# Pre-norm decoder layer with routed experts: the last stage takes x already turned and split, with other buffers, banks and orders

## The reference

```
x = x + self_attention(layernorm(x))                       # 16 heads, Wqkv 512x1536, Wo 512x512
x = x + layernorm(rs * cross_attention(layernorm(x), ctx)) # 16 heads, Wq, Wk, Wv, Wo 512x512
x = x + ffn(layernorm(x))

ffn(x):                       # 2048 tokens
  scores = softmax(x @ gate.T)                             # 64 experts, 8 groups
  keep the 3 best groups, of them the 6 best experts: topk_w, topk_i
  slot = expert * 192 + min(position in the expert, 191)
  buf[slot] = x[token]                                     # 64 x 192 rows
  out = (silu(buf @ Wg.T) * (buf @ Wu.T)) @ Wd.T           # 352 hidden an expert
  y = sum over the 6 choices of out[slot] * topk_w
  shared = (silu(x @ Sg.T) * (x @ Su.T)) @ Sd.T            # 704 hidden
  return y + shared
```

## Time and profile before

| | us |
|---|---|
| median of 3 runs | 1537.34 |
| the profiled execution | 1540.01 |
| its span, first to last instruction | 1538.3 |
| TensorE busy (share of the span) | 1464.2 (95%) |
| VectorE busy | 1115.0 (72%) |
| ScalarE busy | 941.6 (61%) |
| GpSimd busy | 688.1 (45%) |

### The profile page before, as it was taken

How to read it: one execution, slowest core, us unless ns; L and a number is a source line. 1 busy time by engine, 2 the same in 40 slices (tenths; PEclk the granted TensorE clock), 3 DMA queues, 4 the chain that set the end, 5 groups by cost and what they waited for, 6 DMA issues and landing times.

```text
span 1538.3 us, 30281 instructions
## 1 busy us (share of the span) xinstructions
PE 1464.2 (95%) x10344; PEld 1216.4 (79%) x10344; DVE 1115.0 (72%) x1959; ACT 941.6 (61%) x1769; POOL 688.1 (45%) x830
## 2 busy tenths in 40 slices
PE   6999999899999979689999999999999999999988
PEld 4788887678888867578888898888888888876766
DVE  5677676636788788777777777777777777757756
ACT  4556566644656556677777777778777777741110
POOL 2122124342232146355556555555555555347763
PEclk9999999999999999889999999999999999999999
DMA  6012122242121141299877788777887788567664
GB/s 212 1 63 83 37 75 70 73 124 70 56 90 43 43 125 49 88 330 342 283 269 268 264 295 275 271 265 268 298 271 269 268 272 299 193 216 246 191 185 151
DMA packets 116629, 280.25 MB, mean 182 GB/s; under 512 B 17984, under 2 KB 23104, under 8 KB 116544
## 3 DMA queue, kind: packets, MB, share of 16 engines
q1 hardware_dynamic: 98800, 228.25, 43.7%
q0 software_dynamic: 15360, 50.34, 10.7%
q10 hardware_dynamic: 2384, 0.53, 0.2%
HBM read 235.69 MB, written 43.38 MB: 181 GB/s over the span
## 4 chain that ended last, share of the span: by engine, by line
PE 50%; issue 3%; DVE 3%; DVEq 1%; ACT 0%; DMA 0%; SPq 0%
PE e_gu L2615 18%; PE e_gu L2618 9%; PE e_dn_rest L2644 6%; PE e_tr L49 3%; PE e_dn_main L41 3%; PE e_dn_main L43 3%; PE e_dn_main L42 3%; DVE h_acc L2909 1%; DVEq L2938 1%; PE h_dn L41 1%; PE h_dn L42 1%; PE h_dn L43 1%; PE h_gt L41 0%; PE h_gt L43 0%; PE h_gt L42 0%
## 5 line engine op out<-in xcount | busy, mean ns | idle before, releaser
L2377 POOL TENSOR_TENSOR e_hid<-e_h_raw,e_hid 128x256 fp32r<-128x256 f32 (+1 forms) x128 | 128.9, 1007 | 225.7 <-ACT e_hid L2443 225.7
L2615 PE MATMUL e_gu<-e_xT_hi_lo,e_wu 128*128 128x384 f32 (+1 forms) x768 | 223.9, 346 | 0.0
L2615 PE MATMUL e_gu<-e_xT_hi_lo,e_wg 128*128 128x384 f32 (+1 forms) x768 | 221.8, 343 | 0.4 <-issue 0.4
L2618 PE MATMUL e_gu<-e_xT_hi_lo,e_wu 128*128 128x192 f32 (+1 forms) x768 | 157.8, 260 | 0.0
L2385 POOL TENSOR_TENSOR e_wd<-e_raw_d,e_wd 96x512 fp32r<-96x512 f32 x64 | 132.6, 2071 | 55.5 <-ACT e_wd L2427 55.5
L2618 PE MATMUL e_gu<-e_xT_hi_lo,e_wg 128*128 128x192 f32 (+1 forms) x768 | 152.2, 253 | 0.0
L2519 DVE TENSOR_TENSOR e_total<-e_gu,e_low 128x384 f32<-128x384 f32 x192 | 106.1, 553 | 48.3 <-issue 38.9
L2508 DVE TENSOR_TENSOR e_wg<-e_raw_g,e_wg 128x1408 fp32r<-128x1408 f32 x64 | 104.1, 1627 | 45.8 <-ACT e_wg L2418 45.3
L2618 PEld LDWEIGHTS e_gu<-e_xT_hi_lo,e_wg 128*128 128x128 f32 (+1 forms) x768 | 135.2, 180 | 0.0
L2618 PEld LDWEIGHTS e_gu<-e_xT_hi_lo,e_wu 128*128 128x128 f32 (+1 forms) x768 | 134.8, 179 | 0.0
L2439 ACT ACTIVATE e_low<-e_gu 128x384 f32<-128x384 f32 x192 | 93.9, 489 | 59.9 <-issue 49.1
(11 more groups left out here) (427 smaller groups left out, 3941.2 us busy)
## 6 DMA issues: line engine op xcount, KB each, us to landing
e_raw_g<-in_L_ffn_Wg_dram SPq DMA_DIRECT2D x64, 704.0 KB
e_raw_u<-in_L_ffn_Wu_dram SPq DMA_DIRECT2D x64, 704.0 KB
e_raw_d<-in_L_ffn_Wd_dram SPq DMA_DIRECT2D x64, 512.0 KB
y_dram<-e_y_main SPq DMA_DIRECT2D x64, 256.0 KB
e_raw_d<-in_L_ffn_Wd_dram SPq DMA_DIRECT2D x64, 192.0 KB
y_dram<-e_y_rest SPq DMA_DIRECT2D x64, 128.0 KB
s_xr<-in_x_dram SPq DMA_DIRECT2D x16, 256.0 KB
x_dram<-s_x SPq DMA_DIRECT2D x16, 256.0 KB, 2.6
```

What stands on the lines that cost most here:

```text
L2377: pool.tensor_tensor(hid[b][1][:, part, :], h_raw[g.odd][b][:, part, 0:P], hid[b][0][:, part, :].bitcast(F32), ALU.subtract).then_inc(s_hl, 1)
L2615: pe.matmul(gu[(b + c) % 2][0:n, at, 0:2 * CAP], w[b][0][:, k, m:m + n], xT[:, :, k, toks], start=k == 0, stop=False)
L2618: ins = pe.matmul(gu[(b + c) % 2][0:n, at, 0:CAP], w[b][1][:, k, m:m + n], xT[:, 0, k, toks], start=False, stop=k == KC - 1)
```

## The change

- SP stores in cross-attention the two halves of the turned x of the 12 tiles outside AHEAD to `xfT_dram` (two DMAs of 256 KB a tile), and ScalarE's next copy into the single buffer waits for them.
- The last stage loads these halves (two DMAs of 1 MB a turn) into `h_xT` in place of loading xf, turning it and splitting it. The first turn's load is issued in the last expert turn.
- The last matmul of a down tile runs on all 128 rows, with `h_sd`'s first half zeroed in the 64 rows that had been left out.
- Three buffers for gathered rows in place of two, four down banks in place of two.
- VectorE's order of sums and finishes in the last stage is another.
- In every expert half ScalarE splits part 1 of the down weights behind the first SiLU in place of behind the second, and GpSimd's low half of it comes ahead of both low halves of the hidden. In the last expert turn TensorE makes the rest of the down products ahead of the last down product.

```diff
+        def turned_before(t):
+            return len([m for m in range(t) if m // QT != AHEAD])
...
+            def store_turned(t):
+                if t < LAST - 2:
+                    sp.wait_ge(s_er[0], exchanged(0, ("xf", t)))
+                else:
+                    sp.wait_ge(s_fl, t - LAST + 3)
+                at = t % QT * P
+                for half in range(2):
+                    sp.dma_start(route["xfT"][t // QT][half][:, :, at:at + P], fT[half][:].bitcast(F32)).then_inc(s_stT, 16)
...
             for t in range(BATCH + 2):
+                if t >= 3 and (t - 3) // QT != AHEAD:
+                    store_turned(t - 3)
                 if t >= 2:
                     store_x3(t - 2)
...
                 if t:
                     act.wait_ge(s_lg, t)
+                if t and t // QT != AHEAD:
+                    act.wait_ge(s_stT, 32 * turned_before(t))
...
                 if not first:
                     store_main(g.last(), 0)
+                if last:
+                    ahead.load_turned(sp, 0)
...
             def hidden_lo(g, b):
+                down_lo(g, b)
                 for i, part in enumerate(PARTS):
...
-                    if i == 0:
-                        down_lo(g, b)
 
             def down_lo(g, b):
-                pool.wait_ge(s_dh[b], 2 * g.n + 2)
+                pool.wait_ge(s_dh[b], 2 * g.n + 1)
...
                 silu(g, b, 0)
+                d_hi(g, b, 1)
                 low_part(g, b, 1)
...
                 d_hi(g, b, 0)
                 silu(g, b, 1)
-                d_hi(g, b, 1)
                 hidden_hi(g, b, 1)
...
-            ahead.turn_tokens(pe, 0, 2, QT)
+            down_rest(pair(turns - 1))
             down_main(pair(turns - 1), 1)
-            down_rest(pair(turns - 1))
...
+    def load_turned(sp, p):
+        if p == 0:
+            sp.wait_ge(*free["gate_up_before_last"])
+        elif p == 1:
+            sp.wait_ge(*free["raw_down_of_last"])
+        else:
+            sp.wait_ge(s_gu, SCN * (p - 1))
+        for half in range(2):
+            sp.dma_start(xT[p % 2][half][:].bitcast(F32), turned[order[p]][half]).then_inc(s_xt[p % 2], 16)
...
         def gather(n):
-            b = n % 2
-            if n >= 2:
-                pool.wait_ge(s_acc[b], TOPK * (n // 2))
+            b = n % ROWS
+            if n >= ROWS:
+                pool.wait_ge(s_acc[b], TOPK * (n // ROWS))
...
+        dve.memset(sd[0][low_rows, FULL, :].bitcast(F32), 0.0).then_inc(s_wz, 1)
+        early_half, late_half = range(TOPK // 2), range(TOPK // 2, TOPK)
         chunks(0, {2: (0, 0), 3: (0, 1), 4: (1, 0)})
         routed(1, late_half)
         finish(0)
...
-        routed(4)
-        chunks(1, {0: (5, 0), 1: (5, 1), 2: (6, 0), 3: (6, 1), 4: (7, 0)})
-        routed(7, late_half)
+        routed(4, early_half)
+        chunks(1, {0: (4, 1), 1: (5, 0), 2: (5, 1), 3: (6, 0), 4: (6, 1)})
+        routed(7)
         finish(4)
+        finish(5)
         routed(8)
-        finish(5)
-        routed(9)
         finish(6)
         finish(7)
-        routed(10)
-        chunks(2, {1: (11, 0), 2: (11, 1), 3: (12, 0), 4: (12, 1)})
+        routed(9)
+        chunks(2, {1: (10, 0), 2: (10, 1), 3: (11, 0), 4: (11, 1)})
         for c in range(SCN):
             hidden_lo(3, c)
         finish(8)
+        routed(12)
+        finish(9)
         routed(13)
-        finish(9)
-        routed(14)
         finish(10)
         finish(11)
+        routed(14)
         routed(15)
...
                 if n < 2:
                     pe.wait_ge(*free[("main_bank", "rest_bank")[n]])
-                else:
-                    pe.wait_ge(s_o[n % 2], n // 2)
-                toks, bank = slice(t * P, (t + 1) * P), dn[t % 2]
+                elif n >= QT:
+                    pe.wait_ge(s_o[n % 2], (n - QT) // 2 + 1)
+                toks, bank = slice(t * P, (t + 1) * P), dn[t]
...
-                pe.matmul(bank[:], hid_half[late][high_rows, toks], sd[0][high_rows, FULL, :], start=False, stop=True
-                          ).then_inc(s_dn, 1)
+                pe.matmul(bank[:], hid_half[late][:, toks], sd[0][:, FULL, :], start=False, stop=True).then_inc(s_dn, 1)
```

More of the change, by code:

```diff
@@ L920 @@
 AHEAD_SUMS = 6
+ROWS = 3
 COPIED = 4
@@ L2420, in d_hi @@
             def d_hi(g, b, part):
-                if part == 0:
+                if part == 1:
                     act.wait_ge(s_ld[g.odd][b], 32 * (g.uses + 1))
-                f = before(g, b, 2)
-                if f is not None:
-                    act.wait_ge(s_dm, 2 * f[0].n + b + 1)
+                    f = before(g, b, 2)
+                    if f is not None:
+                        act.wait_ge(s_dm, 2 * f[0].n + b + 1)
                 rows, cs = ((P, slice(0, 2)), (96, slice(2, 3)))[part]
@@ L2684, in sb, with shared_programs @@
         return ctx.enter_context(nc.sbuf_tensor("h_" + name, shape, dt))
-    return dict(xf=sb("xf", [P, QT, H]), ones=sb("ones", [P, 1]),
-                idx=[sb(f"idx{b}", [P, TOPK], U32) for b in range(2)], w_t=[sb(f"w_t{b}", [P, TOPK]) for b in range(2)],
-                carry=[sb(f"carry{b}", [P, 1]) for b in range(2)])
-def shared_programs(nc, sems, mine, own, raw, loaded, xf, x3, y_in, out, weight, slot, ident, experts, ahead_hidden):
+    return dict(ones=sb("ones", [P, 1]),
+                idx=[sb(f"idx{b}", [P, TOPK], U32) for b in range(ROWS)], w_t=[sb(f"w_t{b}", [P, TOPK]) for b in range(ROWS)])
+def shared_programs(nc, sems, mine, own, raw, loaded, turned, x3, y_in, out, weight, slot, experts, ahead_hidden):
     order = [q for q in range(BATCH // QT) if q != AHEAD] + [AHEAD]
@@ L2731, in shared_programs @@
         raw_hid = sb("raw_hidden", [P, SCN, QT * P])
-        xf_sb, idx, w_t, carry, ones = (own[k] for k in ("xf", "idx", "w_t", "carry", "ones"))
+        yk.append(sb("yk2", [P, TOPK * H]))
+        idx, w_t, ones = (own[k] for k in ("idx", "w_t", "ones"))
         gt, up = [None, None], [None, None]
@@ L2745, in shared_programs @@
         s_rh = sem("raw_hidden_loaded")
[L2746 to L2749 removed]
+        s_idx = [sem(f"idx_ready{b}") for b in range(ROWS)]
+        s_yk = [[sem(f"rows_gathered{b}_{k}") for k in range(TOPK)] for b in range(ROWS)]
+        s_wt = [sem(f"weights_ready{b}") for b in range(ROWS)]
+        s_acc = [sem(f"routed_sum_step{b}") for b in range(ROWS)]
         s_o = two(sem, "out_ready")
@@ L3050, in feed_forward @@
         experts = expert_programs(nc, sems, wg_in, wu_in, wd_in, xf, table, y, ident, shared_in, raw, loaded, shared)
-        shared_programs(nc, sems, shared, own, raw, loaded, xf, x3, y, out, weight, slot, ident, experts, ahead_hidden)
+        shared_programs(nc, sems, shared, own, raw, loaded, turned, x3, y, out, weight, slot, experts, ahead_hidden)
         ctx.callback(end_phase, nc, sems)
@@ L3117, in build @@
         table = ctx.enter_context(nc.sbuf_tensor("table", [E, CAP + P - REST], F32))
+        xfT = nc.dram_tensor("xfT_dram", [BATCH // QT, 2, P, KC * QT * P], F32, kind="Internal").ap()
+        turned = [[xfT[q, half].rearrange("p (k s) -> p k s", k=KC) for half in range(2)] for q in range(BATCH // QT)]
         ahead_hidden = nc.dram_tensor("hidden_dram", [SCN * P, QT * P], F32, kind="Internal").ap()
```

80 lines of the change are left out of this document (21 added, 59 removed).

## The result

The changed kernel took 1518.83 us (median of 4 runs, 1517.48 to 1519.98), the kernel before 1536.87 beside it (4 runs): a ratio of 0.989, interval 0.9874 to 0.9906. In a later comparison on another chip the same changed kernel took 1529.73 (6 runs, 1526.88 to 1533.2) against 1539.82: 0.9937, interval 0.9919 to 0.9955. It is faster in both; the size of the gain, 18 or 10 us, is what the experiments had to explain.

The account below looks back on a forecast made before the run. TensorE was taken as the bound, a leaky one in the last stage; 27.0 us less, 7.7 more in the loop and 0.5 for the first pair, net 18.8, gave 1521.2 profiled, 1518 median; range 1507 to 1531.

Parts of the forecast that it names:

- the loop: Expert loop: GpSimd's earlier subtraction holds VectorE, so TensorE stops about 0.25 us, 31 times: +7.7 us.
- the first pairs: First expert pair: the down weights are waited for earlier, 0.5 us more.
- Transposes: Last expert turn and last stage: six packets leave TensorE, 4.7 us less, and their own waits, 2.4 us.
- stops: Last stage: the other 10.1 us of TensorE stops nearly vanish, 0.9 us kept, gain 9.2 us.
- clock: Last stage: the slow clock behind two TensorE stops goes with them, gain 3.5 us.
- padding: Down tiles of the last stage: three gaps become 0.24 us, 0.37 us a tile, 16 tiles, gain 5.9 us.
- restarts: TensorE's second matmul behind each stop or transpose packet comes 0.1 us later; about 13 go, gain 1.3 us.
- two buffers, a late gather, a late sum, a late product, a TensorE stop: Last stage: a ring in which VectorE idles 11.4 us for a gather and index copies wait 24.5 us for sums.
- the loop is free: Rival, expert loop: exclusion costs TensorE nothing because 0.2 us of slack appear elsewhere; 1510 us, chance 0.2.
- The row of 614 us: Cross-attention: VectorE's 1.23 us operation ended just when GpSimd's 1.29 us one did, read as excluding each other.
- just in time: End of the last stage: last landing, sums and additions done at 1506 us, TensorE ending near 1507.
- Stores in cross-attention: Cross-attention: 9 us before ScalarE's next copy cover 1 us of issue and a landing of say 5; cost 0.

Follow-up runs that it names:

- e4: Changed kernel with the last product of each down tile on its 64 rows again, without zero padding; 1533.2 us, ratio 0.9954.
- e14: The changed kernel once more, with nothing altered, in the later comparison on another chip; 1529.73 us, ratio 0.9937.
- e5: Changed kernel with two row buffers for the gathers in place of three; 1528.3 us, ratio 0.9909.
- e2: Changed kernel with the old expert order and the finishes of tiles 12 and 13 ahead of the last routed sums; 1519.03 us, ratio 0.9866.
- e3: Kernel before with nothing but the new order in the expert halves; 1546.67 us, ratio 1.0046.

## Why the prediction was right, and where it wasn't

The direction, the median of the first comparison (1518 forecast, 1518.83 measured) and the place of the gain, the last stage, were right. That the median came out within 1 us is partly luck. Between the two profiled executions 18.8 us were forecast and 22.1 measured: the loop was forecast 6.9 us too dear, the first pairs 3.9 and the tail 1.5 too cheap, and the last stage with the last expert turn gained 1.8 more. The medians differ by 18.0 only because the profile before was 3.1 us above its median and the one after 0.8 below.

- *Last stage.* Transposes, stops, clock, padding and restarts: 27.0 forecast, 26.0 measured in the stage and 2.75 in the last expert turn. Padding, the one term that was measured by itself, is exact (5.9, e4). Stops: 11.4 of 12.5 us of waits gone in the first profile; in e14, with the lateness, 7.9 us of waits are there again. The clock is 1.00 throughout 1360 to 1510 us (four windows).
- *The cause of the stops* was half wrong. The step "two buffers, a late gather, a late sum, a late product, a TensorE stop" holds for the stop at 1418.79 of the kernel before (below), and e5 shows VectorE's part of it again. The stop of 3.1 us came from ScalarE's SiLU, 7.1 us late, which I had taken for VectorE's lateness: VectorE was idle for 8.6 us ahead of the product. Three buffers don't cure that. The changed kernel's first profile was without such a loss, which nothing in the prediction had reason to expect, and it reached the forecast; with the loss, in the second comparison, the gain was 10.1 us, and 1529.73 us lies near the upper end of the range (1507 to 1531).

VectorE and TensorE in the kernel before, the first of these two stops:

```profile
1415.98 0.75 DVE L2909 SCALAR_TENSOR_TENSOR h_acc<-h_yk,h_w_t,h_acc 128x512 f32<-128x512 f32 x1 [0.81 <-DMA h_yk<-y_dram,h_idx]
1417.26 0.75 DVE L2909 SCALAR_TENSOR_TENSOR h_acc<-h_yk,h_w_t,h_acc 128x512 f32<-128x512 f32 x1 [0.52 <-DVE h_acc L2909]
1418.04 0.69 DVE L2940 TENSOR_TENSOR h_h_raw<-h_up,h_act_g 128x512 f32<-128x512 f32 x1
...
1418.79 0.50 PE L41 MATMUL h_gt<-h_xT,h_sg 128*128 128x512 f32 x1 [3.16 <-issue]
```

The SiLU had been ready since 1416.3; the product (line 2940) stood behind the sums, and TensorE went on 0.06 us behind it.

- *Expert loop*: +7.7 forecast, +0.8 measured. The mechanism is there, the term was mis-sized: GpSimd held VectorE for 0.44 us and not 0.6, and the slack was 0.46. It came out nearly as "the loop is free", a rival to which I gave 0.2, though not by the way that I named. The row of 614 us, from which I took the exclusion, is of a VectorE operation with one tensor input, not two; line 2546 is the better witness.
- *First pairs*: +0.5 forecast, +4.4 measured up to the third pair (713.97 to 718.34, from first expert products at 648.72 and 648.73). I gave the wait for the down weights no row: in the kernel before ScalarE gets to them at 669.94, and I didn't ask when they had landed. This is the term that was missed by most beside the loop. Where a wait moves ahead of other work, the landing has to be read in the first round too, not only in the steady state.
- *Tail*: TensorE forecast as the end; VectorE ended 2.1 us behind it, +1.5 in the account. The prediction had the gathers "just in time", but the order of the additions, all of tiles 12 to 15 behind the last sums, cost what e2 gives back.
- *Stores in cross-attention*: cost 0 forecast. The first expert product starts at 648.73 in place of 648.72 us. In other profiles it starts up to 2.8 us later, but they are as late at ScalarE's first copy into the buffer already, ahead of any store. From that copy to the product the profiles with the stores take 280.1 to 282.3 us and the two without, before and e3, 280.2 and 282.2: no cost shows above this spread.

## What to carry to other kernels

When a measured total meets the forecast, compare it boundary by boundary all the same: here a loop term 6.9 us too high, first pairs 3.9 us too low, a profile without the lateness and a profile before that was slower than its median made one good number. Measure an engine's start against the end of the one thing that it waits for; that shows lateness which the list of waits puts down to others. And repeat the comparison on a second chip before a gain of 1% is given a size.

## What the runs showed of the hardware

- While GpSimd issues a long run of indirect gathers, ScalarE's next instruction can start up to 13.5 us after all that it waits for is done (11 of 12 profiles), and in some of them TensorE's matmuls start singly, with gaps of up to 1.6 us; in the one profile with plain loads of the same bytes, issued in half the time, neither happens. Last stages with it took 163 to 182 us (other changes in them too), the changed kernel's two profiles 155.6 and 168.0.
- A VectorE operation with two inputs in SBUF that met a GpSimd subtraction took 1.00 in place of 0.56 us and ended 0.42 behind it.
- A product on 64 rows among products on 128 costs 0.37 us in the three gaps around it.
